# A graph layer and expert feed-forward on one core: where a group's sum is turned, and when VectorE adds it

## The reference

```python
xw = x @ W
deg = jax.ops.segment_sum(w, dst, num_segments=n)
dinv = jnp.where(deg > 0, jax.lax.rsqrt(deg), 0.0)
norm = dinv[src] * w * dinv[dst]
out = jax.ops.segment_sum(xw[src] * norm[:, None], dst, num_segments=n)
return out + b
```

## Time and profile before

| | |
|---|---|
| median of three runs | 2776.79 us |
| the profiled execution | 2760.07 us, its span 2758.3 us |
| mean granted TensorE clock | 0.826 |
| TensorE matmul busy | 2008.3 us, 73% of the span |
| TensorE weight load busy | 1397.0 us, 51% |
| GpSimd busy | 1699.3 us, 62% |
| VectorE busy | 899.0 us, 33% |
| ScalarE busy | 424.7 us, 15% |
| group loop of layer 0 | about 517 to 1296 us of the span |
| group loop of layer 1 | about 1308 to 2147 us |

### The profile page before, as it was taken

One profiled execution on the slowest core, in us unless ns is written; L12 is line 12 of the kernel. 1 busy time (PEld: TensorE's weight loads), 2 busy tenths in 40 slices (PEclk: granted clock), 3 DMA queues, 4 the chain that ended last, 5 costly groups with the idle time before them and its releaser, 6 DMA issues.

```text
span 2758.3 us, 29927 instructions
## 1 busy us (share of the span) xinstructions
PE 2008.3 (73%) x8514; PEld 1397.0 (51%) x8515; DVE 899.0 (33%) x2676; ACT 424.7 (15%) x1140; POOL 1699.3 (62%) x1679
## 2 busy tenths in 40 slices
PE   0353249887778886665688888888885473999998
PEld 0251014444445444554445555554554362899997
DVE  7970001111122113342113323232323776333332
ACT  1610000000000000111000000000000465344443
POOL 2887732566656666665765666755665544566665
PEclk6555559988889987878889999998998555999999
DMA  9993013454445443334444545544545313688885
GB/s 321 336 312 101 27 40 124 135 165 152 147 138 168 147 151 103 119 117 119 142 148 143 175 154 170 158 145 141 170 154 186 101 58 129 179 209 207 214 210 137
DMA packets 263529, 431.17 MB, mean 156 GB/s; under 512 B 38800, under 2 KB 147023, under 8 KB 263279
## 3 DMA queue, kind: packets, MB, share of 16 engines
q1 hardware_dynamic: 180591, 253.79, 27.8%
q0 software_dynamic: 81088, 173.80, 23.8%
q10 hardware_dynamic: 1728, 2.13, 0.2%
HBM read 339.36 MB, written 91.16 MB: 156 GB/s over the span
## 4 chain that ended last, share of the span: by engine, by line
another core or an unknown queue 34%; PE 28%; issue 17%; DVE 13%; DMA 3%; ACT 1%; SPq 1%; POOL 1%; DVEq 1%; POOLq 0%; ACTq 0%
PE psum L1508 8%; PE psum L1679 6%; PE psum L1687 6%; PE psum L1554 4%; DVE arena L1122 3%; DMA arena<-pair_weights 1%; DMA out_dram<-ACC 1%; PE psum L1467 1%; SPq L453 1%; PE psum L1670 1%; DVE edge_cols L1214 1%; DVE stats L1220 1%; PE psum L1526 1%; DVE ACC L926 1%
## 5 line engine op out<-in xcount | busy, mean ns | idle before, releaser
L575 POOL DMA_INDIRECT arena<-conv_rows,edge_cols x1120 | 1065.3, 951 | 694.3 <-issue 338.7
L1508 PE MATMUL psum<-arena,X 128*128 128x512 f32 x1568 | 805.7, 636 | 220.5 <-issue 141.4
L1554 PE MATMUL psum<-arena 128*128 128x256 f32 x2240 | 595.3, 399 | 78.2 <-issue 64.8
L1554 PEld LDWEIGHTS psum<-arena 128*128 128x128 f32 x2240 | 447.1, 203 | 271.1 <-issue 218.1
L1508 PEld LDWEIGHTS psum<-arena,X 128*128 128x128 f32 x1568 | 314.6, 202 | 512.8 <-issue 434.4
L1146 DVE TENSOR_TENSOR ACC<-ACC,psum 128x256 f32 x80 | 33.8, 422 | 1037.9 <-remote 441.5
L560 POOL DMA_INDIRECT pair_weights<-scale_b,mean_b x224 | 252.3, 1126 | 116.7 <-issue 67.9
L1122 DVE TENSOR_SCALAR arena<-iota,edge_cols 128x128 f32<-128x128 f32 x1120 | 298.1, 359 | 6.1 <-issue 5.9
L650 POOL DMA_INDIRECT out_dram<-ACC x105 | 166.3, 1583 | 108.9 <-DMA out_dram<-ACC 78.3
L729 ACT ACTIVATE arena<-psum 128x256 f32<-128x256 f32 x80 | 30.4, 380 | 1311.7 <-remote 727.5
L1679 PE MATMUL psum<-ACC,arena 128*128 128x128 f32 x1680 | 208.3, 277 | 0.2 <-DVE ACC L1356 0.2
(11 more groups left out here) (287 smaller groups left out, 1532.4 us busy)
## 6 DMA issues: line engine op xcount, KB each, us to landing
arena<-pair_weights SPq DMA_DIRECT2D x329, 256.0 KB
arena<-in_L_ffn_W_dram SPq DMA_DIRECT2D x113, 512.0 KB, 7.9
pair_weights<-zeros SPq DMA_DIRECT2D x4, 12544.0 KB, 44.2
arena<-conv_rows,edge_cols POOLq DMA_INDIRECT x1120
arena<-pair_weights SPq DMA_DIRECT2D x9, 1792.0 KB
conv_rows<-X SPq DMA_DIRECT2D x14, 896.0 KB
X<-in_x_dram SPq DMA_DIRECT2D x12, 896.0 KB
rows_for_experts<-ACC SPq DMA_DIRECT2D x7, 910.0 KB, 4.2
```

Of the source, the lines that this page charges most:

```text
L575: pool.indirect_dma_start(G[:, n * D:(n + 1) * D], None, y_tab[layer], bass.IndirectOffsetOnAxis(srcT[:, t:t + 1], 0)).then_inc(gathered[n ...
L1508: ins = m.matmul(bank(6 + c, BW), X[:, t * D + c * P:t * D + (c + 1) * P], table, start=(t == 0), stop=(t == NT - 1))
L1554: ins = m.matmul(bank(2 * (k % 2), D), S[:, n * P:(n + 1) * P], G[:, n * D:(n + 1) * D], start=(j == 0), stop=(j == GT - 1))
```

## The change

`SUM_TURN` goes from 2 to 7: TensorE transposes the sum of group k - 1 behind tile 7 of group k (tiles are counted from 0). VectorE's order in group k becomes: wait for `summed` of group k - 1 (that wait now guards the half of `S`), `build(k + 1)`, a block, `add_group(k - 1)`, the shift, the finishes. The last sum is added behind the loop.

```diff
@@ -350,7 +350,7 @@
         SLOT_CH = [(NCH + 1) // 2, NCH // 2]
         FFN_TURNS = (FT - 2) // XSLOTS
         Y_DVE = 4
-        SUM_TURN = 2
+        SUM_TURN = 7
 
         def sliding(row, at, n, step, width):
             a = row[:, at:at + 1]
@@ -1155,15 +1155,19 @@
                                 add_block(blocks)
                                 blocks += 1
                             if k + 1 < GG:
+                                if k:
+                                    dve.wait_ge(summed, GG * layer + k)
                                 build(k + 1)
                             while blocks < NB and (blocks + 1) * NT <= first_unit + units:
                                 add_block(blocks)
                                 blocks += 1
+                            if k:
+                                add_group(k - 1)
                             if layer == 1 and k and 0 in FINISH[1][1][k - 1]:
                                 set_shift(chain_fast)
                             for i in FINISH[layer][1][k]:
                                 finish(layer, i)
-                            add_group(k)
+                        add_group(GG - 1)
                         dve.wait_ge(added, GG * (layer + 1))
                         v.memset(dscr[:, :], 0.0).then_inc(agg_done, 1)
                         finish_rest(layer, NT - len(FINISH[layer][2]), chain_fast)
```

## The result

The changed kernel takes 2818.57 us (median of four runs, 2814.1 to 2822.72) against 2776.32 us (four runs, 2768.07 to 2789.46): ratio 1.0158, interval 1.0119 to 1.0198. It is slower by 42 us. The prediction was 2784 with a range to 2813, and "within 0.5%" as the likeliest case; both were missed, on the slow side. The profiled execution has a span of 2820.9 us where before had 2758.3, 62.6 us more.

What follows compares the result with a forecast made beforehand. The prediction took TensorE's updates, seen only after a train of gathers, to set the cadence. Middle of layer 0, its end and layer 1 gave 0 + 17 - 10 = +7 us: 2767 profiled, 2784 median, range 2745 to 2813.

Steps and rivals of the forecast that it cites:

- within 0.5%: Whole kernel: losses at the end of layer 0 about made good, or no effect, 2763 to 2791 us; chance 0.45.
- what sets the cadence: Both group loops: a TensorE update late in a train of gathers is seen only when the train is over.
- the filled stall: TensorE before the turn: 4.13 us and its like filled with 5.6 us of work, worth 0 on the cadence.
- the middle of layer 0: Groups 3 to 26, no linears: 0 taken, bounds -14 to +21 us.
- the end of layer 0: Groups 27 to 37: linear behind tile 8 waits behind the add, 65 us for three groups, +17 us, bounds -2 to +18.
- the price of a double train: Two groups' gathers without a pause: 34.8 + 4.7 = 39.5 us, including TensorE's crawl until some 4 us after the train.
- the gain of layer 1: Five double trains each up to 2 us shorter: -10 us, bounds -20 to +10.
- the cadence is near 20 us whichever way the trains fall: Group loops: 59.5 us for three groups, double plus single, against 60.4 for three single trains.
- What the trace was to show: Turn stall gone or small, 28-gather trains, third linear stalled, copies 40 to 45 us apart, loops within 20 us of today.
- Slower, VectorE's new order: Rival: linear behind tile 8 caught behind the add after a double train, 2795 to 2816 us; chance 0.32.

Runs made afterwards that it cites:

- e1: Kernel before with only the turn moved behind tile 7 (behind tile 2 where a new block's units begin), VectorE's order as before: 2425.81 us against 2425.56.
- e2: Kernel before with only VectorE's new order, the turn staying behind tile 2: 2426.54 us against 2425.56.
- e5: The changed kernel, not edited, run again in the experiments' session: 2425.93 us against 2423.43 for the kernel before.
- e4: Changed kernel, with GpSimd waiting until its last gathers have landed before it starts the next group's train: 2626.99 us, ratio 1.0840.
- E10: Kernel before, sums copied only when the next train has landed, eight small memsets as a fixed pause between trains: 2585.59 us, ratio 1.0670.
- E11: Changed kernel, sums and masks held until the next train has landed, eight small memsets as a fixed pause between trains: 2569.24 us, ratio 1.0603.
- E6: Kernel before, each train waiting for the last one's landing, sums copied only when the next train has landed: 2725.57 us, ratio 1.1255.
- E7: Changed kernel, each train waiting for the last one's landing, sums and masks held until the next train has landed: 2632.58 us, ratio 1.0864.
- E12: Kernel before, with trains in pairs made by waits, and copies and adds held until a pair has landed: 2695.08 us, ratio 1.1123.
- E8: Changed kernel, with trains in pairs made by waits, and copies, masks and adds held until a pair has landed: 2633.58 us, ratio 1.0864.
- E9: Changed kernel with finishes ahead of the add, trains in pairs made by waits, copies, masks and adds held until a pair landed: 2577.59 us, ratio 1.0645.
- e3: Changed kernel with the group's finishes put ahead of the add of the last sum: 2427.05 us against 2425.56 for the kernel before.

## Why the prediction was wrong

**Right: what sets the cadence.** A late update of TensorE, not TensorE, released the trains. Where updates are prompt the kernel is 350 us faster and the change is worth nothing (e1, e2, e5); where a pause stands between trains it costs its length (e4).

**Right: the filled stall is worth about 0 in single trains.** E10 and E11 differ by 0.6%. E6 and E7 seemed to refute it, and were shown to measure something else.

**Right in size: the middle of layer 0.** 0 was taken (bounds -14 to +21); it is +6. The reason beside it was off: with the five units that a group has there, three groups are 150 records and not 162, and a turn that goes from tile 2 to tile 7 passes one unit and not two.

**Right in kind, mis-sized: the end of layer 0.** From the turn that is seen only after the train to the third linear the chain came as written. But the term was +17 us (65 us for three groups, bounds to +18), and it is +28 by the gathers (68.2 us for three groups). What was short was the price of the double train: I let the sum come at 44 us, and two groups took 1220.15 - 1172.21 = 47.9 us, 2 us by the later add and 2 us on TensorE's way behind it at the lower clock.

**The step that failed: the price of a double train.** The prediction took "34.8 + 4.7 = 39.5 us for two groups", and from it both the gain of layer 1 ("each becomes up to 2 us shorter", -10 us) and "the cadence is near 20 us whichever way the trains fall". Layer 1 shows 45.5 us a pair, so each further double train costs 5 us instead of nothing, and ten instead of five turned -10 into +27. The rows for it stood beside the argument. The double train of the earlier trace rows takes 12.4 + 28.7 = 41 us, the prediction said so. The one that ends in the earlier trace rows begins behind this copy of the kernel before:

```profile
1348.12 0.38 ACT L729 ACTIVATE arena<-psum 128x256 f32<-128x256 f32 x1 [46.41 <-remote]
```

That is 1392.69 - 1348.12 = 44.6 us for two groups, and the five of that loop average 46.4. The mean of the loop had it too: from its first train to its last it takes 811.4 us for 39 groups, 20.8 us each and not the "0.5 us" above 20.0 that the bound of -20 took (the 20.2 us each of "1618 us for 80 groups" is low because the stretch of layer 0 in the earlier trace rows starts with group 2). I priced the pair from a model of records (crawl until 4 us after the train) when the trace had it measured, and left out that the releases of the dense table's buffers come late like every other update (6.6 us, and 7.28 us of TensorE's time, at 1622.73).

**What the trace was to show.** The stall at the turn went, trains of 28 gathers formed between 1050 and 1255 us, and TensorE stood before the third linear, as said. Two signs failed: the copies around a double train are up to 48.1 us apart instead of 40 to 45, and the two loops together differ by 61 us from before instead of by under 20.

**The rival that came true, in part by a wrong name.** "Slower, VectorE's new order", 2795 to 2816, had 0.32 and is nearest the result. The condition that I gave for it, "from the point where a train is double", was the right one, and the wait that it names is there. But E12 shows that the old kernel loses more in a double train than the changed one. What harms is that double trains form where there were none. At the end of layer 0 (groups 28 to 37) the sums of the kernel before are over 12.0 to 13.5 us into a train, and all trains are single; in the changed kernel they are over at 9.9 to 10.6 us where the train becomes double and at 11.2 us where it does not. That the sums are earlier because of the moved turn (26 records from it to the sum there, where 48 stood), and not because of the order, is argued and was not tried at 2776 us: I could not bring that state of the updates back.

The sum by the rows: 0 + 17 - 10 = +7 was forecast; +6, +28, +3 (the passage between the layers, which the sum did not have) and +27 make +64 by the gathers, and the span grew by 62.6. The +28 is explained by a chain that E8 and E9 reproduce. The +27 rests on reading two traces; no run of these separates the crawl from the late loads in it.

## What to carry to other kernels

An engine's stall that you fill is worth what the next release behind it is worth: follow the buffer that it frees to the engine that sets the cadence before you count a gain, and price a pattern that the trace already shows by its measured length, not by a model of it. In a queue served in order, work that frees a buffer for a faster engine belongs ahead of work that waits for that engine: in the held double trains of E8 and E9 the finishes ahead of the add were worth 56 us. And a probe that adds a wait measures also what that wait hangs on: the landings of E6 looked like a gain of 93 us. Whether the changed kernel with the finishes first would beat the kernel before at 2776 us was not measured; where updates are prompt it doesn't (e3).

## What was not expected of the hardware

- The same kernel takes 2776 us in the first measurements and 2421 to 2426 us in those of the experiments. In the traces of the first the updates of TensorE that fall late in a train of GpSimd's gathers are seen up to 21 us late (turn 1190.48, add 1212.13), and TensorE spaces single records by 2.1 us (1631.11, 1633.21, 1635.31); in those of the experiments neither was seen. Not all of the difference lies in the two loops: the first gather of layer 0 starts at 461.95 us in the first trace of the changed kernel and at 378.71 in that of E5, so 83 of the 399 us between their spans are already there before it. The cause is open: a difference of the chips or of what runs beside the kernel would fit, and no run here tells them apart.
- The prediction's count of records from the start of a train does not settle when an update is seen. For it: in the changed kernel the turn of 1602.15, early in its train, is added at 1602.67, at once, and the one of 1627.85, in a double train's second half, at 1637.03, when the train was over. Against it: it had 36 records as 1.6 us late, while the sum of group 32 above has 35 and is 7.9 us late, and that of group 8 in layer 1 has 28 (the last ones at 1548.49, its train from 1536.69) and is copied 7.1 us late, after the train. The time since the train's start sorts the sums no better. What decides was not found. TensorE and ScalarE around the sum of group 8:

```profile
1548.49 1.03 PE L1558 MATMUL psum<-arena 128*128 128x256 f32 x4
...
1556.64 0.38 ACT L729 ACTIVATE arena<-psum 128x256 f32<-128x256 f32 x1 [11.38 <-remote]
```

- The landing of a train's last gathers took 2.5 us, and 4.7 us where loads of 256 KB ran beside it with the DMA share at 0.76 to 0.81.
